# Two graph layers on one core: parts of a threshold search moved from VectorE to GpSimd, and the work between the two steps dealt in another order

## The chip, the core and the metric

The kernel runs on one core of a Trainium2 chip. The metric is the device time of one launch in microseconds (us); smaller is better. TensorE multiplies, VectorE (DVE in the rows) and ScalarE (ACT) do elementwise work and reductions, GpSimd (POOL) does small elementwise work and issues some DMAs, and SyncE (SP) issues the other DMAs. Each engine takes its instructions in the order of the program; between engines there are only semaphores.

## The reference

`x` is 3327 x 256, `adj` is a sparse symmetric 3327 x 3327 matrix. All is float32.

```python
h = relu(layernorm(x))
S = adj + eye
Rf = S / rowsum(S);  Rb = S / colsum(S)[:, None]
Xf = Xb = Xa = h;  Z = 0
for s in range(2):                       # step one, step two
    logits = (Xa @ W1) @ W2 @ (Xa @ W3).T
    # per row: keep the largest logits until their softmax mass reaches 0.9,
    # then softmax over the kept ones
    A = nucleus_softmax(logits, 0.9)
    Xf = Rf @ Xf;  Xb = Rb @ Xb;  Xa = A @ Xa
    Z += Xf @ U1[s] + Xb @ U2[s] + Xa @ U3[s]
x = x + layernorm(h + Z) * gamma + beta
h = relu(layernorm(x))
x = x + attention(h)                     # second layer, 8 heads
```

## The kernel before

Rows are padded to 3328 and cut into 26 tiles of 128 rows (t = 0 to 25). A step works through the tiles one after another, with tile t + 1 being begun while tile t is searched and tile t - 1 is used. For every tile, in a step:

- TensorE makes the logits (L1100), ScalarE copies them to SBUF (L1344), VectorE takes the row's maximum (`row_max`, L1871 in step two), ScalarE the exponentials (L1351).
- ScalarE probes two thresholds over the whole row (`probe`, L1404 and L1410, twice each) and signals `searched_early` at the end (L1433 in step two). In step two a bracket (its ends are the pairs `high` and `deep`, each a threshold and the excess mass there) is tightened with the first probe by GpSimd (`bracket`, L1724 to L1733) and with the second by VectorE.
- VectorE searches on: `start_search` makes the next candidate from the bracket, `bisect(t, k)` weighs the mass above the candidate in one pass over the row (`weigh`, L1928; three passes in step one, five in step two), and moves the candidate by a step from a small table (`steps_of`). In step two the pass k = 0 is followed by `narrow` (L1935 to L1942), and GpSimd makes the table (`make_steps`, L1738). In step one VectorE makes the table itself (`spans`, L1881), right before the first pass.
- `threshold` (L1967 to L1992) finds the exact threshold among the largest 24 values below the candidate; `sum_larger` (L1997 to L2000) signals `larger_summed`. GpSimd then counts (`count_needed`, L1743 to L1755), ScalarE counts ties (L1451) and lifts the row (L1457), GpSimd settles (`settle`: L1760, L1763 signals `settled`, L1766 signals `totalled`), and VectorE, which waits for both, makes the kept row (`keep`, L2109 to L2117).
- TensorE transposes the kept row and multiplies it with the features, and multiplies the adjacency tile (L1118).

VectorE's order in step two, from tile 2 on, is: `start_search(t)`, `bisect(t, 0)`, `keep(t-1)`, `row_max(t+1)`, `bisect(t, 1)` to `bisect(t, 4)`, `threshold(t)`, `sum_larger(t)`. GpSimd's order is `prepare(t+1)`, `bracket(t+1)`, `count_needed(t)`, `settle(t)`, `make_steps(t+1)`, then three DMA issues that add the tile's results to z in HBM.

**Between the steps** lies a stage of 26 slots. In slot t TensorE transposes a tile (L763) and multiplies it with U1 and U2 (L777, eight matmuls, into two PSUM banks of four), ScalarE scales the second bank into `both` (L818, L819), and VectorE sums four scaled parts into z (`gather`, L853 to L861: two from the first bank, then two from `both`); GpSimd adds z to HBM with a DMA (L1803). TensorE may refill the first bank of slot t for slot t + 2 when L855 of slot t has run (`sides_read`), the second when L819 has (`both_ready`). Step two's tiles 0 and 1 are searched in between the slots, so all engines deal slots and passes by an order written out by hand. TensorE does tile 0's adjacency products (L1118) and the first logits there too.

## Time and profile before

| what | value |
|---|---|
| median of 3 runs | 2296.23 us (2295.15 to 2298.56) |
| the profiled execution | 2297.46 us |
| its span | 2295.7 us |
| mean granted TensorE clock | 0.983 of full speed |
| busy: TensorE, VectorE, ScalarE, GpSimd | 2140.1, 2042.6, 1935.1, 854.2 us |
| step one | about 60 to 900 us, 32.2 us a tile |
| between the steps | about 1005 to 1155 us |
| step two after it | about 1155 to 2220 us, 42.75 us a tile |

Busy time alone doesn't say which engine sets the end: TensorE is busy most, but the chain that ended last can run through another. A row of the timeline gives the start, the length, the engine, the line, and in square brackets how long the engine had been idle before it and what ended that.

### The profile page before, as it was taken

What the parts mean: (1) busy time and instruction counts of PE and PEld (TensorE: products, weight loads), DVE (VectorE), ACT (ScalarE), POOL (GpSimd) and SP (SyncE); (2) the same over time, 40 slices, a digit from 0 to 9 for tenths busy, and PEclk for the clock granted to TensorE, in tenths of its full rate; (3) what the DMA queues carried; (4) which work ended last, traced back from release to release, by engine and by line L of the source; (5) the groups of instructions that cost most, each with busy time, mean ns of one, the idle gap of its engine ahead of it and who ended that gap; (6) DMA issues with size and microseconds to landing.
All of it is one profiled execution on the core that took longest, in us unless ns stands there. A gap on an engine that the chain in (4) does not pass through costs nothing.

```text
span 2295.7 us, 26397 instructions
## 1 busy us (share of the span) xinstructions
PE 2140.1 (93%) x8282; PEld 1381.0 (60%) x8282; DVE 2042.6 (89%) x3758; ACT 1935.1 (84%) x2831; POOL 854.2 (37%) x1233
## 2 busy tenths in 40 slices
PE   7599999999999998998899999999999999999987
PEld 4377777777777777543355555555555555555556
DVE  5699999999999998138859999999999999999996
ACT  5899999999999996258379989989989999899844
POOL 2134443344334442003224444444444444444420
PEclk9699999999999999999999999999999999999998
DMA  7255544554455543332322112112212212122242
GB/s 247 79 124 138 113 98 112 129 115 110 101 124 129 114 100 72 105 99 42 54 56 57 39 52 57 44 48 57 52 40 56 52 42 54 52 44 52 54 124 72
DMA packets 85168, 190.05 MB, mean 83 GB/s; under 512 B 12193, under 2 KB 65056, under 8 KB 85024
## 3 DMA queue, kind: packets, MB, share of 16 engines
q0 software_dynamic: 26208, 61.37, 17.1%
q1 hardware_dynamic: 56496, 125.48, 16.5%
q10 hardware_dynamic: 2320, 1.48, 0.2%
q8 instruction: 67, 1.10, 0.2%
q14 instruction: 77, 0.63, 0.1%
HBM read 154.19 MB, written 34.10 MB: 82 GB/s over the span
## 4 chain that ended last, share of the span: by engine, by line
DVE 45%; PE 4%; issue 1%; POOL 0%; ACT 0%; DVEq 0%; ACTq 0%; POOLq 0%
DVE junk L1928 19%; DVE small L1975 4%; DVE logits L1967 4%; DVE logits L2117 4%; DVE small L1871 4%; PE bank L1118 2%; DVE small L1956 1%; DVE small L1959 1%; PE bank L777 1%; DVE small L1980 1%; DVE small L1983 1%; DVE QT L2031 1%; PE bank L1181 1%; PE bank L1144 0%; PE bank L1100 0%
## 5 line engine op out<-in xcount | busy, mean ns | idle before, releaser
L1928 DVE SCALAR_TENSOR_TENSOR junk<-logits,small,expd 128x3327 uint8<-128x3327 f32 x184 | 677.9, 3684 | 4.7
L1144 PE MATMUL bank<-h_aug,turns 128*128 128x256 f32 x2704 | 628.2, 379 | 0.0
L1118 PE MATMUL bank<-both,pair 128*128 128x512 f32 x1352 | 611.2, 596 | 17.8 <-ACT sides L1497 17.8
L1144 PEld LDWEIGHTS bank<-h_aug,turns 128*128 128x128 f32 x2704 | 498.4, 190 | 94.5 <-issue 30.1
L1118 PEld LDWEIGHTS bank<-both,pair 128*128 128x128 f32 x1352 | 251.0, 190 | 302.6 <-issue 261.0
L1118 PE MATMUL bank<-h_aug,both 128*128 128x257 f32 x1352 | 316.6, 384 | 2.8 <-ACT sides L1480 1.6
L1118 PEld LDWEIGHTS bank<-h_aug,both 128*128 128x128 f32 x1352 | 250.9, 190 | 64.5 <-issue 26.9
L1100 PE MATMUL bank<-KTr,QT 64*128 64x512 f32 (+1 forms) x728 | 246.5, 613 | 43.7 <-ACT logits L1344 39.8
L1404 ACT ACTIVATE junk<-expd,small 128x3327 int8<-128x3327 f32 x88 | 270.1, 3069 | 1.5
L1410 ACT ACTIVATE junk<-expd,small 128x3327 int8<-128x3327 f32 x88 | 270.5, 3073 | 0.3
L1473 ACT ACTIVATE turns<-bank 128x512 f32<-128x512 f32 (+1 forms) x364 | 188.7, 562 | 52.0 <-PE bank L1134 46.5
L1134 PE MATMUL bank<-ident,logits 128*128 128x128 f32 x1352 | 190.8, 277 | 39.6 <-DVE logits L2117 29.4
L1743 POOL TENSOR_TENSOR small<-small 128x1 f32<-128x1 f32 x52 | 14.5, 278 | 571.5 <-DVE small L2000 571.5
L1134 PEld LDWEIGHTS bank<-ident,logits 128*128 128x128 f32 x1352 | 159.8, 141 | 100.2 <-DVE logits L2117 39.9
L1975 DVE MAX8 small<-logits 128x8 f32<-128x416 f32 (+1 forms) x416 | 209.9, 578 | 0.0
L1451 ACT ACTIVATE junk<-logits,small 128x3327 int8<-128x3327 f32 x52 | 159.4, 3066 | 49.1 <-DVE small L1992 49.1
L1100 PEld LDWEIGHTS bank<-KTr,QT 64*128 64x128 f32 x728 | 90.0, 188 | 182.5 <-ACT logits L1344 104.4
L1967 DVE SCALAR_TENSOR_TENSOR logits<-logits,small,expd 128x3327 f32<-128x3327 f32 x44 | 162.6, 3695 | 1.5
L1351 ACT ACTIVATE expd<-logits,small 128x3327 f32<-128x3327 f32 x44 | 135.0, 3069 | 34.0 <-DVE small L1873 33.9
L1344 ACT ACTIVATE logits<-bank 128x512 f32<-128x512 f32 (+1 forms) x286 | 145.4, 575 | 20.7 <-PE bank L1100 20.6
L2117 DVE SCALAR_TENSOR_TENSOR logits<-logits,small,expd 128x3328 f32<-128x3328 f32 x42 | 154.7, 3684 | 4.8 <-DVE small L2114 0.5
L1708 POOL TENSOR_SCALAR small<-small 128x1 f32<-128x1 f32 x52 | 40.9, 787 | 264.4 <-ACT expd L1351 243.1
(263 smaller groups left out, 3097.8 us busy)
## 6 DMA issues: line engine op xcount, KB each, us to landing
both<-adj_turned SPq DMA_DIRECT2D x52, 832.0 KB, 6.8
both<-adj_turned POOLq DMA_DIRECT2D x52, 832.0 KB, 9.3
pair<-adj_turned SPq DMA_DIRECT2D x52, 832.0 KB, 4.5
z<-sides POOLq DMA_DIRECT2D x78, 128.0 KB, 3.2
spread<-sides POOLq DMA_DIRECT2D x26, 128.5 KB, 3.6
turns<-spread SPq DMA_DIRECT2D x26, 128.5 KB, 2.1
attended<-att_out SPq DMA_DIRECT2D x26, 128.0 KB, 8.5
expd<-attended SPq DMA_DIRECT2D x26, 128.0 KB, 2.1
```

The costliest lines, as they stand in the source:

```text
L1100: pe.matmul(logits_bank(i)[:, 0:w], QT[r:r + DA, bass.ts(t, P)], keys_of(n, w), start=True, stop=True).then_inc(sem["logits_done"], 1)
L1118: done = pe.matmul(SX[:, 0:width], half(t, h)[:, bass.ts(jj, P)], rows_of(j), start=(j == 0), stop=(j == T - 1))
L1134: last = pe.transpose(TB[i % NTB][:, bass.ts(b, P)], kept[:, bass.ts(g + b, P)], ident[:, :])
L1144: last = pe.matmul(AB[:, 0:D], attT[i % 4][:, b, :], h_aug[:, g + b, 0:D], start=(g + b == 0), stop=(g + b == T - 1))
L1404: chain.did(act.activation(junk2[:, 0:N], e, ACT.Relu, bias=at, scale=-0.5, accum_out=col(t, "tail")))
L1410: chain.did(act.activation(junk2[:, 0:N], e, ACT.Sign, bias=at, scale=-0.5, accum_out=col(t, "side")))
L1451: act.activation(junk2[:, 0:N], me, ACT.Sign, bias=col(t, "tau"), scale=-1.0, accum_out=col(t, "less")).then_inc(sem["ties_counted"], 1)
L1473: act.activation(attT[i % 4][:, 0:w, :], TB[i % NTB][:, 0:w * P].rearrange("q (b r) -> q b r", r=P), ACT.Relu).then_inc(sem["turned_stored ...
L1928: chain.did(dve.scalar_tensor_tensor(junk[:, 0:N], logits[t % 3][:, 0:N], col(t, "cand"), expd[t % NE][:, 0:N], ALU.is_gt, ALU.mult, accum ...
L1967: chain.did(dve.scalar_tensor_tensor(me[:, 0:N], logits[t % 3][:, 0:N], col(t, "cand"), expd[t % NE][:, 0:N], ALU.is_le, ALU.mult, accum_o ...
L1975: chain.did(dve.max(winners(t)[:, 8 * n:8 * n + 8], me[:, at:min(at + NP // SEGMENTS, N)]))
L2117: dve.scalar_tensor_tensor(kept, kept, col(t, "sharetau"), expd[t % NE][:, :], ALU.add, ALU.min).then_inc(sem["kept_ready"], 1)
```

## The change

Five things, in the words of the code:

1. In step two the bracket's second tightening goes from VectorE to GpSimd (`close_bracket`, nine operations in four dependent groups). VectorE's `start_search` waits for `closed` and begins with the reciprocal. The first three tightening operations change places.
2. In step two `narrow` goes to GpSimd, nine operations in four dependent groups with the table's at the end. It waits for `weighed`, the end of the pass k = 0; VectorE waits for `steps_ready` ahead of the pass k = 1.
3. In step one GpSimd makes the table of steps (`make_steps`), after `prepare`; VectorE waits for it behind its first pass.
4. Between the steps ScalarE begins z: a third operation in its slot, from `both` in SBUF, which waits for its own L819 and for the z buffer to be free. VectorE's `gather` has three operations instead of four and waits for `z_begun`.
5. Between the steps VectorE's list has tile 1's start after slot 16 as before, but its passes k = 0, 1, 2 and `keep(0)` stand two slots apart.

```diff
@@ store_products(t), ScalarE
                act.activation(both[:, t, D:2 * D], bank[:, D:2 * D], ACT.Copy, scale=col_inv[:, t:t + 1]
                               ).then_inc(mid["both_ready"], 1)
+                act.wait_ge(mid["both_ready"], t + 1)
+                if t < 4:
+                    act.wait_ge(mid[f"z_stored{t}"], stores_in(t))
+                else:
+                    act.wait_ge(mid[f"z_added{t % 4}"], t // 4 * 16)
+                act.activation(z_out[t % 4], both[:, t, 0:D], ACT.Copy, scale=row_inv[:, t:t + 1]
+                               ).then_inc(mid["z_begun"], 1)
@@ gather(t), VectorE
-                dve.wait_ge(mid["products_done"], 2 * t + 1)
...
-                chain.did(dve.tensor_scalar(z, sides[:, 0:D], row_inv[:, t:t + 1], None, ALU.mult))
+                dve.wait_ge(mid["z_begun"], t + 1)
+                chain.did(dve.scalar_tensor_tensor(z, sides[:, 0:D], row_inv[:, t:t + 1], z, ALU.mult, ALU.add))
...
-                dve.wait_ge(mid["both_ready"], t + 1)
-                chain.did(dve.scalar_tensor_tensor(z, both[:, t, 0:D], row_inv[:, t:t + 1], z, ALU.mult, ALU.add))
-                chain.wait()
@@ GpSimd; move_ends holds the eight operations of bracket, which now calls it
+                    def close_bracket(t):
+                        high, deep = pair(t, "high"), pair(t, "deep")
+                        pool.wait_ge(sem["searched_early"], t + 1)
+                        move_ends(t, pair(t, "point1"), high, deep)
+                        pool.tensor_tensor(pair(t, "width"), deep, high, ALU.subtract).then_inc(sem["closed"], 1)
+
+                    def narrow(t):
...
+                        pool.wait_ge(sem["weighed"], t + 1)
+                        pool.wait_ge(sem["closed"], t + 1)
+                        chain.did(pool.tensor_tensor(up, deep, high, ALU.add))
+                        chain.did(pool.tensor_scalar(col(t, "move"), col(t, "mass"), col(t, "target"), None, ALU.is_ge))
+                        chain.did(pool.tensor_tensor(bottom, point, deep, ALU.subtract))
+                        chain.did(pool.tensor_scalar(half, pair(t, "width", 0), -0.5, None, ALU.mult))
+                        chain.wait()
+                        chain.did(pool.tensor_scalar(excess, point, -2.0, up, ALU.mult, ALU.add))
+                        chain.did(pool.tensor_scalar(col(t, "cand"), bottom, -0.5, col(t, "cand"), ALU.mult, ALU.add))
+                        chain.wait()
+                        chain.did(pool.tensor_scalar(moved, excess, col(t, "move"), bottom, ALU.mult, ALU.add))
+                        chain.did(pool.tensor_scalar(col(t, "cand"), half, col(t, "move"), col(t, "cand"),
+                                                     ALU.mult, ALU.add))
+                        chain.wait()
+                        pool.tensor_scalar(steps_of(t), constants[:, 4:4 + 2 * late], moved, None, ALU.mult
+                                           ).then_inc(sem["steps_ready"], 1)
 
                     def make_steps(t):
...
+                        pool.wait_ge(sem["low_ready"], t + 1)
+                        pool.tensor_scalar(steps_of(t), constants[:, 4:4 + 2 * late], col(t, "low"), -0.5 ** early,
+                                           ALU.mult, ALU.mult).then_inc(sem["steps_ready"], 1)
@@ GpSimd's list, between the steps and then per tile
+                            if t == 7:
+                                close_bracket(0)
                             if t == 8:
-                                make_steps(0)
+                                pool.wait_ge(sem["setup"], 2 * late)
+                                narrow(0)
...
                             if t == 15:
+                                close_bracket(1)
                                 count_needed(0)
                             if t == 16:
                                 settle(0)
-                                make_steps(1)
+                                narrow(1)
...
                             prepare(t + 1)
-                            if not first_step:
+                            if first_step:
+                                make_steps(t + 1)
+                            else:
                                 bracket(t + 1)
+                                close_bracket(t + 1)
                         if first_step or t > 0:
                             count_needed(t)
                             settle(t)
                             if not first_step and t + 1 < T:
-                                make_steps(t + 1)
+                                narrow(t + 1)
@@ VectorE's list between the steps
                         sum_larger(0)
-                        slot(15)
+                        slots(15, 17)
                         start_search(1)
-                        slot(16)
+                        slot(17)
                         bisect(1, 0)
-                        slot(17)
+                        slots(18, 20)
+                        keep(0)
+                        slot(20)
                         bisect(1, 1)
-                        slot(18)
-                        keep(0)
-                        slot(19)
+                        slots(21, 23)
                         bisect(1, 2)
-                        slots(20, T)
+                        slots(23, T)
                         bisect(1, 3)
```

VectorE's instructions in step two, at the start of a tile's search (`sum_larger` of the tile before is L2000), before:

```order
L2000 SCALAR_TENSOR_TENSOR small<-small,s_ones 128x24
L1896 TENSOR_SCALAR s_mask<-small 128x1
L1897 TENSOR_SCALAR s_mask<-small 128x1
L1900 COPY_PREDICATED small<-s_mask,small 128x2
L1901 COPY_PREDICATED small<-s_mask,small 128x2
L1903 TENSOR_TENSOR small<-small 128x2
...
L1906 RECIPROCAL small<-small 128x1
```

and in the changed kernel, where L1920 is the reciprocal of `start_search`, L1938 the pass k = 0 and L2107 the first instruction of `keep`:

```order
L1998 SCALAR_TENSOR_TENSOR small<-small,s_ones 128x24
L1920 RECIPROCAL small<-small 128x1
L1922 TENSOR_SCALAR small<-small 128x1
L1925 TENSOR_SCALAR small<-small 128x1
L1927 SCALAR_TENSOR_TENSOR small<-small 128x1
L1930 SCALAR_TENSOR_TENSOR small<-small 128x1
L1933 TENSOR_SCALAR small<-small 128x1
L1938 SCALAR_TENSOR_TENSOR junk,small<-logits,small,expd 128x3327
L2107 RECIPROCAL small<-small 128x1
```

The six operations ahead of the reciprocal, two behind L1933 and the five of `narrow` behind the pass are gone from VectorE.

GpSimd's instructions at the same place in the changed kernel, from the end of `count_needed` (L1777) over `settle` (L1782 to L1788) and `narrow` (L1743 to L1755) to the first DMA; before, `settle` was followed by L1738 alone and then by the DMA:

```order
L1777 TENSOR_SCALAR small<-small 128x1
L1782 TENSOR_SCALAR small<-small 128x1
L1785 TENSOR_SCALAR small<-small 128x1
L1788 TENSOR_SCALAR small<-small 128x1
L1743 TENSOR_TENSOR small<-small 128x1
L1744 TENSOR_SCALAR small<-small 128x1
L1745 TENSOR_TENSOR small<-small 128x1
L1746 TENSOR_SCALAR small<-small 128x1
...
L1755 TENSOR_SCALAR small<-s_constants,small 128x10
L1803 DMA z<-sides 128x256
```

So the queue behind `settle` has eight more instructions ahead of the DMAs.

VectorE's instructions between the steps in the changed kernel, from tile 1's pass k = 0 to `keep(0)` (L2107): slots 18 and 19 stand between them with three operations on z each, where before there were slot 17, the pass k = 1 and slot 18.

```order
L1938 SCALAR_TENSOR_TENSOR junk,small<-logits,small,expd 128x3327
L847 TENSOR_SCALAR row_sum<-turns 128x1
L849 RECIPROCAL row_inv<-row_sum 128x1
L856 SCALAR_TENSOR_TENSOR sides<-bank,row_inv,sides 128x256
L858 SCALAR_TENSOR_TENSOR sides<-bank,col_inv,sides 128x256
L861 SCALAR_TENSOR_TENSOR sides<-both,col_inv,sides 128x256
L847 TENSOR_SCALAR row_sum<-turns 128x1
...
L2107 RECIPROCAL small<-small 128x1
```

The passes moved back in the list; the slots moved forward.

## Rows read from the trace of the kernel before

**Rows 1.** The page's chain that ended last, shares of the span by engine

```profile
DVE 45%; PE 4%; issue 1%; POOL 0%; ACT 0%; DVEq 0%; ACTq 0%; POOLq 0%
```

**Rows 2.** Busy us (x instructions) by engine in one stretch of step two

```profile
1400.00:1500.00 100.00, 96.74 (x333) 55.61 (x332) 96.28 (x184) 90.50 (x132) 45.02 (x70) 1.00 0.21 51
```

**Rows 3.** Timeline of VectorE in step two: start, length, engine, line, operation

```profile
1410.61 0.15 DVE L1896 TENSOR_SCALAR s_mask<-small 128x1 int32<-128x1 f32 x1
...
1411.45 0.16 DVE L1906 RECIPROCAL small<-small 128x1 f32<-128x1 f32 x1
...
1412.92 3.69 DVE L1928 SCALAR_TENSOR_TENSOR junk<-logits,small,expd 128x3327 uint8<-128x3327 f32 x1
...
1417.47 0.16 DVE L2109 RECIPROCAL small<-small 128x1 f32<-128x1 f32 x1
...
1418.12 3.69 DVE L2117 SCALAR_TENSOR_TENSOR logits<-logits,small,expd 128x3328 f32<-128x3328 f32 x1
1421.72 3.61 DVE L1871 TENSOR_REDUCE small<-logits 128x1 f32<-128x3327 f32 x1
```

**Rows 4.** Timeline of GpSimd over the same stretch

```profile
1411.68 0.27 POOL L1748 TENSOR_SCALAR small<-small 128x1 f32<-128x1 f32 x1
1412.04 0.23 POOL L1751 TENSOR_SCALAR small<-small 128x1 f32<-128x1 f32 x1
...
1412.57 0.23 POOL L1755 TENSOR_SCALAR small<-small 128x1 f32<-128x1 f32 x1
1413.67 3.12 POOL L1760 TENSOR_SCALAR small<-small 128x1 f32<-128x1 f32 x1 [0.87 <-ACT junk L1451]
1416.88 0.29 POOL L1763 TENSOR_SCALAR small<-small 128x1 f32<-128x1 f32 x1
1417.28 0.34 POOL L1766 TENSOR_SCALAR small<-small 128x1 f32<-128x1 f32 x1
```

**Rows 5.** Timeline of step one, a reduction on VectorE and GpSimd beside it

```profile
527.81 2.29 DVE L1856 TENSOR_REDUCE small<-logits 128x1 f32<-128x2048 f32 x1
528.81 0.31 POOL L1760 TENSOR_SCALAR small<-small 128x1 f32<-128x1 f32 x1
```

**Rows 6.** Timeline of GpSimd, first and last of `bracket`'s eight operations

```profile
1186.47 0.22 POOL L1724 TENSOR_SCALAR small<-small 128x1 f32<-128x1 f32 x1 [9.36 <-ACT small L1433]
1188.10 0.20 POOL L1733 TENSOR_TENSOR small<-small 128x2 f32<-128x2 f32 x1
```

**Rows 7.** Timeline of ScalarE in step two: the second probe's last operation

```profile
1450.04 0.39 ACT L1433 ACTIVATE small<-small 128x1 f32<-128x1 f32 x1
```

**Rows 8.** Timeline of step one, VectorE and ScalarE

```profile
523.13 0.21 DVE L1889 TENSOR_SCALAR small<-small 128x1 f32<-128x1 f32 x1
523.25 0.22 DVE L1881 TENSOR_SCALAR small<-s_constants,small 128x6 f32<-128x6 f32 x1
523.51 3.69 DVE L1928 SCALAR_TENSOR_TENSOR junk<-logits,small,both 128x3327 uint8<-128x3327 f32 x1
...
532.07 3.07 ACT L1351 ACTIVATE expd<-logits,small 128x3327 f32<-128x3327 f32 x1 [0.24 <-DVE small L1873]
```

**Rows 9.** Timeline of VectorE between the steps: tile 0's search begins, and tile 2's

```profile
1051.86 0.15 DVE L1896 TENSOR_SCALAR s_mask<-small 128x1 int32<-128x1 f32 x1 [2.90 <-ACT small L1433]
...
1195.81 0.16 DVE L1896 TENSOR_SCALAR s_mask<-small 128x1 int32<-128x1 f32 x1 [13.14 <-ACT small L1433]
```

**Rows 10.** Groups by line, 1000 to 1160 us: count, busy us, mean ns, idle before

```profile
L853 DVE TENSOR_SCALAR sides<-bank,row_inv 128x256 f32<-128x256 f32 x26 | 12.6, 483 | 6.3 <-PE bank L777 6.0 <-DVE row_inv L842 0.3
L819 ACT ACTIVATE both<-bank,col_inv 128x256 f32<-128x256 f32 x26 | 12.2, 471 | 0.0
```

**Rows 11.** Timeline of TensorE between the steps

```profile
1111.57 3.60 PE L777 MATMUL bank<-logits,turns 128*128 128x512 f32 x8
...
1121.93 5.37 PE L777 MATMUL bank<-logits,turns 128*128 128x512 f32 x8 [2.66 <-DVE sides L855]
...
1128.42 1.96 PE L777 MATMUL bank<-logits,turns 128*128 128x512 f32 x4 [0.91 <-DVE sides L855]
```

87 lines of the change are left out of this document (25 added, 62 removed).

## The prediction

> **What bounds the kernel now.** I read the chain that ended last first: 45% of the span on VectorE against 4% on TensorE [rows 1], although TensorE is busier. It reaches back only to the stage between the steps, so step one has to be judged by who waits there. The busy times of a stretch of step two show VectorE at 96.28 of 100 us and TensorE at 96.74 [rows 2]: the first has no listed idle time in a tile's 42.75 us, only the small gaps between dependent instructions, the second has some 1.4 us a tile left. So VectorE sets step two's pace, and TensorE lies close behind. In step one ScalarE waits 0.24 us for VectorE in each tile, just ahead of the exponentials [rows 8]: VectorE sets the pace there too. Between the steps the engines wait for each other in turn: TensorE waits for VectorE's slots [rows 11], VectorE for ScalarE's probe [rows 9].
>
> **Step one.** The table of steps is one VectorE operation, 523.25 to 523.47, and the pass starts 0.04 later, at 523.51 [rows 8]. Without it the pass follows L1889, which ends at 523.34, so at 523.38: 0.13 us less. GpSimd makes the table right after `prepare`, most of a tile ahead of its use, so that costs nothing; its cover is most of a 32 us tile, and if it were gone VectorE would wait out one small operation. ScalarE's 0.24 us become 0.11, still above zero. 26 tiles x 0.13 = **3.3 us**. From below: nothing, if ScalarE's 0.24 were not slack at all.
>
> **Step two, what VectorE sheds.** At the start of a search the six operations ahead of the reciprocal take 1410.61 to 1411.45, 0.84 us, and the two behind L1919 hold the pass back by 0.13, by the same step as in step one [rows 3, 8]: the pass starts at 1411.95 instead of 1412.92. Behind the pass, from its end (1416.61) to `keep` (1417.47) lie 0.86 us, nearly all of it `narrow` [rows 3]. Together 1.8 us a tile. Most of it doesn't arrive, and this is the core of the forecast.
>
> **What is late next: `settle`.** `keep` waits for `settled`. GpSimd's L1760 took 3.12 us, from 1413.67 to 1416.79, and the pass on VectorE ended at 1416.61 [rows 3, 4]. The same L1760 took 0.31 us beside a row reduction [rows 5]. So a VectorE pass with two operands in SBUF holds back a GpSimd operation begun under it, a reduction doesn't. The Trainium skill says this in "SBUF — State Buffer", section "Who interferes with whom": the two share a port as an exclusive lock, a Vector instruction with two SBUF inputs shuts out a GpSimd one that reads SBUF, `tensor_reduce` never does. By that rule the trace agrees, with 3.12 against 0.31 us.
>
> Now replay GpSimd with the pass at 1411.95. `count_needed` is released by `sum_larger`, which doesn't move. L1748 begins at 1411.68 and gets through; L1751 would begin at 1412.04 [rows 4], 0.09 us after the pass, and is held until the pass ends at 1411.95 + 3.69 = 1415.64, so it ends near 1415.7. From L1751's end to L1755's end are 0.53 us (1412.27 to 1412.80): 1416.25. L1760 starts 0.1 later with 0.31 us of its own: 1416.65. L1763 ended 0.38 after L1760 (1416.79 to 1417.17): 1417.03, and `keep` begins 0.1 us behind that, at 1417.13 instead of 1417.47. `totalled` follows 0.45 after `settled`, as before, so the kept row's own start stays 0.65 behind `keep`: 1417.78 instead of 1418.12. Of 1.8 us, **0.34** arrive; about 1.4 become a wait of VectorE ahead of `keep`, in which the pass is over and GpSimd is free.
>
> **Do the new GpSimd chains come in time?** `narrow` begins behind L1766, near 1417.5. One group of four gets in partly before the kept row's 3.69 us; the rest runs from 1421.5 on, under the row maximum, a reduction that ends at 1425.3 [rows 3]. Eight operations in three groups took 1.83 us [rows 6], so what is left needs some 2 us of 3.8. `close_bracket` has the eight and one more, 2.2 us with the signal; the second probe ends at 1450.43 [rows 7], so `closed` comes at 1452.7, while the reciprocal would want to start at 1410.61 + 42.75 = 1453.36. Both hidden, with 1.8 and 0.7 us to spare. The DMAs behind `narrow` go out some 5 us later; their readers stand one tile on. If a cover goes, the excess is paid in full.
>
> Tile 2's search waits 13.14 us for ScalarE anyway [rows 9]; there `close_bracket` stands open (2.2 instead of 0.84 us) and `narrow`'s going pays it back, so I take nothing. Tiles 3 to 25: 23 x 0.34 = **7.8 us**.
>
> **Between the steps.** A slot of VectorE loses one operation of 0.48 and its gap, 0.52 us [rows 10]. A slot of ScalarE gains one; no row shows it, so 0.38 (small operations nearby, an estimate: L1433's 0.39 [rows 7]) to 0.47 (L819 [rows 10]), and 0.15 for waiting on L819: about 0.5. Five such slots (3 to 7) lie ahead of tile 0's second probe, for which VectorE already waits 2.90 us at 1051.86 [rows 9]. That search begins 5 x 0.5 + (2.2 - 0.84) = 3.8 us later. Seven slots at 0.52 and `narrow`'s 0.8, less about 1 us for a first `steps_ready` that nothing covers, win back nearly that much by slot 14; TensorE's product 16, which waits for slot 14, comes 0.3 later.
>
> Then the dealing. TensorE waited 2.66 us for slot 18, and the eight matmuls behind took 5.37 us instead of 3.60 [rows 11]: 1.2 GHz for part of them after the idle time, where full clock gives 3.60. Slot 19 cost 0.91 more. Together 2.66 + 1.77 + 0.91 = 5.3 us. With the first pass behind slot 17 and two slots from pass to pass, VectorE needs 2 x 1.74 + 4.3 = 7.8 us for two slots and a pass (1.74: three operations of 0.48 on z with their gaps and 0.2 to 0.3 for the row's inverse; 4.3: the pass of 3.69 and two small operations behind it; both estimates from those rows [rows 3, 10]), TensorE 2 x 3.65 = 7.3 (3.60 less its overlap, and two transposes): slots 18 to 22 are read in time, and only the product after the third pass waits, for about 1.1. 5.3 - 1.1 - 0.3 = **3.9 us**. From there TensorE's products lead to the first logits, and these to step two, so it arrives. Bounds: 0 if the new waits fall so that two more products run at the lower clock, 6 if the early part costs nothing.
>
> **Sum.** 3.3 + 7.8 + 3.9 = 15.0. The profiled execution took 2297.46, which gives 2282.5; the median lies 1.2 below that execution, so **2281.5**.
>
> **Rivals.**
>
> A. *`settle` slips through earlier.* If the pass starts 0.1 us later than I have it, L1751 runs and only L1754 and L1755 are held; `settled` comes 0.3 us sooner. 23 x 0.3 = 7 more: 2274.5. For it: only 0.09 us lie between. Against it: the two starts are as regular as clockwork from tile to tile. 0.17.
>
> B. *Moving work to GpSimd buys nothing in step two.* If L1748 is held as well, `settled` is 0.36 later and the 0.34 us are gone; the same if `close_bracket` is slowed by more than its 0.7 us, as VectorE's small two-operand instructions run beside it. Then 3.3 + 3.9 remain: 2289. The Trainium skill warns of it in "Perfetto Trace Analysis", section "Optimizing Scalar/DVE Operations": as the two share a read port, moving operations between them might not help. Here the trace agrees for most of it, with 1.4 of 1.8 us. 0.15.
>
> C. *ScalarE's share of z costs TensorE.* `sides_read` now needs ScalarE too, which sits in 3 us probes. If two or three more products wait as long as the 2.66 us and run at the lower clock, 6 us are lost instead of 3.9 won: 2291.5. For it: the waits of 2.66 us [rows 11]. Against it: `both_ready` tied TensorE to ScalarE already. 0.12.
>
> D. *The table of steps comes late* (slower). One place: VectorE ahead of the pass k = 1. It decides once `narrow` needs more than the 3.8 us under the row maximum, or is held there after all. Then its 2 us stand open: 23 x (2 - 0.34) = 38 lost, 7 won: 2327. Against it: 0.31 us beside the reduction [rows 5]. 0.06.
>
> The forecast itself 0.5, own range 2277 to 2286.
>
> **Numbers.** A measurement here can tell about 0.2%, 4.6 us: faster is below 2291.6. The forecast, A, B and half of C are faster: 0.84, which I take down to 0.81 for parts that add up against me; same 0.12, slower 0.07. The range reaches from A's 2273 to C's 2292.
>
> **What would show it.** Right: in step two a period of 42.4 us, no small VectorE operations around the pass, a wait of about 1.4 us ahead of `keep` for GpSimd, its L1751 successor about 3.6 us long; step one's tile 0.13 shorter; no wait of TensorE at slots 18 and 19. Wrong: VectorE waiting for `closed` or for `steps_ready` in steady tiles, or products at the lower clock behind slot 20.

## The result and the profile after

The changed kernel takes 2277.32 us in the median (2276.47 to 2278.12, 4 runs), the kernel before 2295.81 beside it (2295.15 to 2298.56, 4 runs): ratio 0.9917, 95% interval 0.9905 to 0.9928, 18.5 us less. The prediction was 2281.5 us, range 2273 to 2292. Sign and range held; the two terms of step one and step two were both mis-sized, in opposite directions.

First the page of the changed kernel: busy time by engine, and the chain that ended last by engine.

```profile
PE 2137.1 (94%) x8282; PEld 1379.3 (61%) x8282; DVE 1987.0 (87%) x3368; ACT 1947.4 (86%) x2857; POOL 1137.5 (50%) x1701
DVE 74%; PE 8%; issue 6%; POOL 4%; ACT 4%; DMA 0%; DVEq 0%; SPq 0%; ACTq 0%; POOLq 0%
```

VectorE lost 56 us of work, GpSimd gained 283, much of it waiting that the profile counts as busy: a held small operation is listed with 3.4 us. GpSimd now has 4% of the chain [rows 1].

Where the time went can be read from how far apart the same instructions stand in the two profiled executions. The row maximum of step two (L1871 before, L1902 after) gives it: the rows list the instructions of one line from 1190 us on, with their durations in ns and the first and the last start; before, then after. The first start is tile 3's, the last tile 25's.

```profile
L1871 DVE TENSOR_REDUCE small<-logits x23: 3609/3610/3619, 1207.9 to 2148.5; 128x1 f32<-128x3327 f32 x23
```

```profile
L1902 DVE TENSOR_REDUCE small<-logits x23: 3603/3604/3606, 1201.5 to 2125.9; 128x1 f32<-128x3327 f32 x23
```

940.6 us became 924.4 over 22 tiles: 42.75 became 42.02 a tile, 0.74 less, where the prediction had 0.34. The rest, by the same reading:

| stretch of the profiled executions | before | after | difference |
|---|---|---|---|
| to step one's last search | 877.7 | 876.7 | -1.0 |
| from there to tile 0's row maximum | 139.8 | 136.9 | -2.9 |
| tile 0's row maximum to tile 2's (the slots) | 146.4 | 143.2 | -3.2 |
| tile 2's row maximum to tile 3's | 44.0 | 44.7 | +0.7 |
| 22 tiles of step two | 940.6 | 924.4 | -16.2 |
| behind the last row maximum | 147.2 | 148.8 | +1.6 |

The second line is not the change's: it touches nothing there, and in the experiments below, which share that code, the same stretch took 136.8 to 140.4 us. The third line is loose too: kernels that are alike between the steps (runs 9 and 10 below) took 143.1 and 142.0 us there. The profiled pair is 21 us apart; the runs say 18.5.

Now a steady tile of step two in the changed kernel, VectorE from the last small operation ahead of the pass k = 0 to the row maximum [rows 3]:

```profile
1444.20 0.21 DVE L1933 TENSOR_SCALAR small<-small 128x1 f32<-128x1 f32 x1
1444.45 3.70 DVE L1938 SCALAR_TENSOR_TENSOR junk<-logits,small,expd 128x3327 uint8<-128x3327 f32 x1
1448.08 0.08 DVE L1938 DVE_READ_ACCUMULATOR junk<-logits,small,expd 128x1 f32 x1
1449.26 0.16 DVE L2107 RECIPROCAL small<-small 128x1 f32<-128x1 f32 x1 [1.11 <-POOL small L1785]
...
1449.97 3.73 DVE L2115 SCALAR_TENSOR_TENSOR logits<-logits,small,expd 128x3328 f32<-128x3328 f32 x1
1453.63 3.60 DVE L1902 TENSOR_REDUCE small<-logits 128x1 f32<-128x3327 f32 x1
```

and GpSimd over the same stretch [rows 4]: the end of `count_needed` (L1770 to L1777), `settle` (L1782, L1785), then `narrow`.

```profile
1444.13 0.27 POOL L1770 TENSOR_SCALAR small<-small 128x1 f32<-128x1 f32 x1
1444.49 0.23 POOL L1773 TENSOR_SCALAR small<-small 128x1 f32<-128x1 f32 x1
1444.81 3.43 POOL L1776 TENSOR_SCALAR small<-small 128x1 f32<-128x1 f32 x1
1448.21 0.23 POOL L1777 TENSOR_SCALAR small<-small 128x1 f32<-128x1 f32 x1
1448.54 0.31 POOL L1782 TENSOR_SCALAR small<-small 128x1 f32<-128x1 f32 x1
1448.94 0.29 POOL L1785 TENSOR_SCALAR small<-small 128x1 f32<-128x1 f32 x1
...
1450.04 0.20 POOL L1745 TENSOR_TENSOR small<-small 128x1 f32<-128x1 f32 x1
1450.19 3.60 POOL L1746 TENSOR_SCALAR small<-small 128x1 f32<-128x1 f32 x1
...
1455.28 0.34 POOL L1755 TENSOR_SCALAR small<-s_constants,small 128x10 f32<-128x10 f32 x1
```

The reader is to see three things. VectorE waits 1.11 us ahead of `keep`, for `settled`. L1773, which the prediction had held, began 0.04 us behind the pass and ran in 0.23 us, and so it did in all 23 tiles from tile 3 on; the next, L1776, is held to the pass's end in each of them. `narrow` is held in the same way under the kept row and is done 1.8 us ahead of its reader.

### The profile page after: what moved, and what is told of

Its sections match the earlier page's. It is cut to its first block, busy times and chain, and to the rows that moved or that the text cites. A ratio compares the mean times of both kernels' runs of the same rounds, so it can differ in the third digit from the quotient of the medians.

```text
span 2274.7 us, 26450 instructions
## 1 busy us (share of the span) xinstructions
PE 2137.1 (94%) x8282; PEld 1379.3 (61%) x8282; DVE 1987.0 (87%) x3368; ACT 1947.4 (86%) x2857; POOL 1137.5 (50%) x1701
## 4 chain that ended last, share of the span: by engine, by line
DVE 74%; PE 8%; issue 6%; POOL 4%; ACT 4%; DMA 0%; DVEq 0%; SPq 0%; ACTq 0%; POOLq 0%
DVE junk L1938 28%; DVE small L1973 9%; DVE logits L1965 8%; DVE logits L2115 8%; DVE small L1902 4%; DVE small L1887 3%; DVE small L1954 2%; PE bank L754 2%; PE bank L777 2%; DVE small L1957 2%; DVE small L1978 2%; POOL small L1776 1%; DVE small L1981 1%; DVE logits L1894 1%; PE bank L1110 1%
## 5 line engine op out<-in xcount | busy, mean ns | idle before, releaser
L1938 DVE SCALAR_TENSOR_TENSOR junk<-logits,small,expd 128x3327 uint8<-128x3327 f32 x184 | 678.2, 3686 | 8.1 <-POOL small L1755 3.5
L1719 POOL TENSOR_SCALAR small<-small 128x1 f32<-128x1 f32 x52 | 34.1, 656 | 256.7 <-ACT small L1425 256.7
L1343 ACT ACTIVATE expd<-logits,small 128x3327 f32<-128x3327 f32 x44 | 135.1, 3071 | 18.5 <-DVE small L1904 18.3
```

The costliest lines, as they stand in the source:

```text
L1938: return dve.scalar_tensor_tensor(junk[:, 0:N], logits[t % 3][:, 0:N], col(t, "cand"), expd[t % NE][:, 0:N], ALU.is_gt, ALU.mult, accum_ou ...
```

## The experiments

Theory S, which is the prediction's core: in step two `settled` is what ends late. A GpSimd operation that begins behind the start of a two-operand pass of VectorE waits out the pass, so `settled` comes as many small groups behind the pass's end as are left when it begins, and what is taken off VectorE is worth only what it moves that. Several of the expectations call it theory L. A group is a set of GpSimd operations that don't depend on each other; each group waits for the one before. The rivals are named run by run. Each run was timed beside the kernel before; the ratios compare with 0.9917.

**1. The bracket's ends back on VectorE.**

```diff
@@ close_bracket, GpSimd
-   move_ends(t, pair(t, "point1"), high, deep)
-   pool.tensor_tensor(pair(t, "width"), deep, high, ALU.subtract).then_inc(sem["closed"], 1)
+   pool.sem_inc(sem["bracketed"], 1)
@@ start_search, VectorE: the six operations ahead of the reciprocal, as before
+   chain.did(dve.copy_predicated(high, mask[:, 0:1].to_broadcast([P, 2]), here))
...
+   dve.tensor_tensor(pair(t, "width"), deep, high, ALU.subtract).then_inc(sem["closed"], 1)
```

> The changed kernel with the bracket's last move given back to VectorE (the six small operations ahead of the reciprocal); narrow stays on GpSimd. Theory S (settle is what ends late): the pass k = 0 starts 0.86 us later in a tile of step two, but then all of count_needed gets through ahead of it, so settled comes only 0.26 us later (pass end + 0.5 instead of pass end + 1.1), and the tile goes from 42.0 to 42.3 us: 23 x 0.26 = 6 us, less about 1 between the steps, so some 5 us more than the changed kernel, near 2282.5, ratio 0.9943. Rival N (the gain of step two is narrow's, which lay on the path behind the pass; the earlier pass buys nothing): no difference from the changed kernel, 2277. Rival P (every operation shed counts): 0.86 x 23 = 20 us more, near 2297.

Measured: 2280.85 us, ratio 0.9928 (0.9915 to 0.9942), 2.5 us above the changed kernel by the ratios. The tile takes 42.27 us, 0.25 more; tile 0's row maximum to tile 2's takes 140.7 instead of 143.2. All of `count_needed` now runs ahead of the pass, and one operation is held:

```profile
1443.87 0.22 POOL L1776 TENSOR_SCALAR small<-small 128x1 f32<-128x1 f32 x1
1445.04 2.91 POOL L1781 TENSOR_SCALAR small<-small 128x1 f32<-128x1 f32 x1 [0.94 <-ACT junk L1444]
1448.04 0.29 POOL L1784 TENSOR_SCALAR small<-small 128x1 f32<-128x1 f32 x1
```

The pass now starts 2.11 us behind the last accumulator of `sum_larger`, where it was 1.32. So 0.79 us of VectorE's work cost 0.25: theory S, and neither N (nothing) nor P (all of it). The size in total was a miss: between the steps 2.5 us came back, not 1. Tile 0's search accounts for 1.5 of them; the other 1.0 comes at slot 16, where runs 9 and 10, which are alike there, differ by 1.2.

**2. `narrow` back on VectorE.**

```diff
@@ bisect, k = 0, VectorE
-   weigh(t).then_inc(sem["weighed"], 1)
+   chain.did(weigh(t))
+   chain.wait()
+   narrow(t)          # the five operations of before; two more stand ahead of the pass again
@@ narrow, GpSimd
+   pool.wait_ge(sem["narrowed"], t + 1)   # and then the table alone
```

> The changed kernel with narrow given back to VectorE (with the two differences ahead of the pass; GpSimd only makes the table); the bracket's ends stay on GpSimd. Theory S: VectorE waits 1.1 us for settled behind the pass anyway, and narrow's 0.86 us fit into that wait. The pass starts 0.13 later, so 0.1 us a tile, 3 us in 23 tiles; the last tile loses its 2.1 us wait for the table and pays 0.9, and tile 0 does the same: about 2 less. Near 2278.5, ratio 0.9926; the wait ahead of keep is 0.2 to 0.3 us. Rivals N and P: 0.86 to 1.0 us a tile, 20 to 23 us more, near 2298.

Measured: 2280.01 us, ratio 0.992 (0.9907 to 0.9934), within the measurement of the changed kernel. The tile takes 42.23 us, 0.21 more and not 0.1. VectorE's timeline, from `narrow`'s last operation to the kept row:

```profile
1451.34 0.21 DVE L1936 SCALAR_TENSOR_TENSOR small<-small 128x1 f32<-128x1 f32 x1
1451.97 0.16 DVE L2113 RECIPROCAL small<-small 128x1 f32<-128x1 f32 x1 [0.42 <-POOL small L1769]
```

`narrow` lies whole in the wait for `settled`, with 0.42 us left. What its move to GpSimd bought in a steady tile is only the 0.2 us by which small operations ahead of the pass no longer hold it back: the same group is the first one held in both kernels, so `settled` moves with the pass, one for one. The move also costs at the ends: with `narrow` on VectorE the last tile is 2.0 us shorter (146.8 us behind the last row maximum instead of 148.8), and the stretch from tile 0's row maximum to tile 2's took 1.4 us less (141.8, of which 1.0 comes at the same slot 16), against 4.6 us lost in 22 tiles. Rivals N and P are out: they gave 20 us.

**3. z begun by VectorE again.**

```diff
@@ store_products, ScalarE
-   act.activation(z_out[t % 4], both[:, t, 0:D], ACT.Copy, scale=row_inv[:, t:t + 1]).then_inc(mid["z_begun"], 1)
@@ gather, VectorE: four operations, as before
+   chain.did(dve.tensor_scalar(z, sides[:, 0:D], row_inv[:, t:t + 1], None, ALU.mult))
```

> The changed kernel with z begun by VectorE again, as in the kernel before; all else as changed. Theory E (the slots pass the work from one busy engine to another): VectorE's slots 0.52 us longer, ScalarE's 0.5 shorter, VectorE no longer waits 36 us for ScalarE's z; tile 0's probes come 2.5 us sooner, seven slots of VectorE cost 3.6: within 2 us of the changed kernel, 2277 (2275 to 2279). Rival V (VectorE's slots were the bound, so z on ScalarE is worth 0.5 us a slot from slot 8 on): some 6 to 9 us more, near 2284. Rival C (ScalarE's z costs TensorE waits): 4 us less, 2273.

Measured: 2277.99 us, ratio 0.991 (0.9896 to 0.9923). From tile 0's row maximum to tile 2's it takes 143.1 us, against 143.2. Theory E: the move is worth nothing that can be seen. ScalarE's z operation takes 0.51 us, VectorE's took 0.48, and between the steps VectorE waits 36 us for it.

**4. The old dealing.**

```diff
@@ VectorE's list between the steps: pass, keep and slots in the order of before
-   slots(15, 17); start_search(1); slot(17); bisect(1, 0); slots(18, 20); keep(0); slot(20); bisect(1, 1)
+   slot(15); start_search(1); slot(16); bisect(1, 0); slot(17); bisect(1, 1); slot(18); keep(0); slot(19)
```

> The changed kernel with tile 1's search, passes and keep(0) dealt among the slots as in the kernel before. Theory K (as predicted): TensorE waits for slots 18 and 19 again, 2.7 + 0.9 us, and the eight matmuls behind the first wait take 1.8 us more at the lower granted clock; with the wait that the later dealing has (1.36 us) gone, about 4 us more than the changed kernel, 2281, ratio 0.9936. Rival Z (z on ScalarE has shortened the slots so far that the old dealing does as well): no difference, 2277, and no wait of TensorE over 1 us there.

Measured: 2282.4 us, ratio 0.9932 (0.9918 to 0.9945), 3.4 us above the changed kernel; the stretch takes 147.2 instead of 143.2 us. TensorE's timeline has the two waits of the kernel before [rows 11], the first with 4.29 us instead of 2.66:

```profile
1119.49 5.08 PE L777 MATMUL bank<-logits,turns 128*128 128x512 f32 x8 [4.29 <-DVE sides L858]
1125.44 3.67 PE L777 MATMUL bank<-logits,turns 128*128 128x512 f32 x8 [0.65 <-DVE sides L858]
```

The granted clock from 1119 to 1125 us is 0.72 of full, where the changed kernel has 1.00. Theory K; 4.0 us for the dealing by the profiles and 3.4 by the runs, where the prediction had 3.9 net of what the early part loses. One word on the change: in the kernel before, as in this run, tile 1's search begins behind slot 15; in the changed kernel it begins behind slot 16, so it too stands one slot later.

**5. A reduction in place of the first pass.**

```diff
@@ bisect, k = 0, step two
-   weigh(t).then_inc(sem["weighed"], 1)
+   dve.tensor_reduce(col(t, "mass"), logits[t % 3][:, 0:N], AX.X, ALU.max).then_inc(sem["weighed"], 1)
```

> The changed kernel, but the first pass of step two's search is a row reduction (tensor_reduce, one operand, 3.6 us) in place of the two-operand pass of 3.7 us; the mass it should find is not computed, so the thresholds of step two are not the reference's, while the count and length of all other instructions stay. Theory L (a two-operand pass holds GpSimd's operations back, a reduction doesn't): the operation of count_needed that took 3.43 us takes 0.2 to 0.3, settled is there before the pass ends, and VectorE's 1.1 us wait ahead of keep is gone. The kept row can then start when ScalarE's lift is done, 0.8 us sooner; TensorE has only 0.5 us a tile left, so the tile goes from 42.0 to 41.5 us: 22 x 0.5 = 11 us less, near 0.987 of the kernel before. Rival G (GpSimd's chain is late of itself, whatever VectorE does): the long operation stays long or the wait stays, 42.0 us a tile, 0.9917.

This kernel leaves out the mass that the pass should find. Measured: 2258.22 us, ratio 0.9826 (0.9811 to 0.9841). GpSimd's timeline, under a reduction from 1442.55 to 1446.17:

```profile
1442.91 0.24 POOL L1776 TENSOR_SCALAR small<-small 128x1 f32<-128x1 f32 x1
1443.11 0.22 POOL L1777 TENSOR_SCALAR small<-small 128x1 f32<-128x1 f32 x1
1444.29 0.31 POOL L1782 TENSOR_SCALAR small<-small 128x1 f32<-128x1 f32 x1 [0.95 <-ACT junk L1443]
1444.69 0.29 POOL L1785 TENSOR_SCALAR small<-small 128x1 f32<-128x1 f32 x1
```

L1776 takes 0.24 us in place of 3.43, in all 22 tiles of the stretch, and `settled` is there 1.2 us ahead of the reduction's end. That is theory L as clearly as it can be had. The Trainium skill says in "SBUF — State Buffer", section "Who interferes with whom", that on this chip `tensor_reduce` never contends with GpSimd; the trace agrees. The expectation was wrong on what comes next: it let TensorE stop the gain at 0.5 us a tile, and it is 0.83 (41.19 us a tile). The kept row now waits for ScalarE's lift, the only wait of VectorE that is listed in a steady tile:

```profile
1447.26 3.69 DVE L2116 SCALAR_TENSOR_TENSOR logits<-logits,small,expd 128x3328 f32<-128x3328 f32 x1 [0.64 <-ACT logits L1449]
```

**6. One more small group on GpSimd.**

```diff
@@ count_needed, behind the first subtraction of need
+   if not first_step:
+       chain.did(pool.tensor_scalar(col(t, "spare"), col(t, "need"), 1.0, 0.0, ALU.mult, ALU.add))
+       chain.wait()
```

> The changed kernel with one more small operation in step two's count_needed, on which the next one waits (0.3 us more on GpSimd; its result is used by nothing). Theory L: the operation that now begins 0.04 us after the pass and gets through begins 0.3 us after it and is held to the pass's end; one group more is left to run behind the pass, so settled comes 0.35 us later and the tile takes 42.35 instead of 42.0: 23 x 0.35 = 8 us more than the changed kernel, ratio 0.995. Rival G (the 0.3 us are absorbed while the pass runs, as the chain has 3.7 us of pass to run in): no difference, 0.9917.

Measured: 2285.74 us, ratio 0.9948 (0.9935 to 0.9962), 7 us above the changed kernel. VectorE's wait ahead of `keep` went from 1.11 to 1.42 us, the tile from 42.02 to 42.33:

```profile
1447.96 3.48 POOL L1776 TENSOR_SCALAR small<-small 128x1 f32<-128x1 f32 x1
1451.53 0.24 POOL L1779 TENSOR_SCALAR small<-small 128x1 f32<-128x1 f32 x1
```

L1776, which is the changed kernel's L1773, now begins 0.31 us behind the pass (1447.65) and is held. One operation, 0.3 us with its gap and ahead of a wait of 3.5 us, is paid in full.

**7. `count_needed` shortened.**

```diff
@@ count_needed
+   pool.wait_ge(sem["tau_ready"], t + 1)
+   chain.did(pool.tensor_tensor(col(t, "floor"), col(t, "target"), col(t, "negabove"), ALU.add))
+   chain.did(pool.tensor_scalar(col(t, "negtau"), col(t, "tau"), -1.0, None, ALU.mult))
+   chain.wait()
+   pool.wait_ge(sem["gt_summed"], t + 1)
+   chain.did(pool.tensor_tensor(col(t, "need"), col(t, "floor"), col(t, "gt"), ALU.subtract))
...
-   chain.did(pool.tensor_tensor(col(t, "need"), col(t, "target"), col(t, "have"), ALU.subtract))
-   chain.wait()
...         # -tau no longer stands in the last group
@@ sum_larger, VectorE: the sum of the larger values now signals by itself
+   dve.scalar_tensor_tensor(kept, v, col(t, "tau"), v, ALU.is_gt,
+                            ALU.mult, accum_out=col(t, "gt")).then_inc(sem["gt_summed"], 1)
```

> The changed kernel with GpSimd's count_needed shortened: target + negabove and -tau are computed as soon as tau is there, the first subtraction starts when the larger values are summed, 0.23 us ahead of their count, and one group of dependent operations falls away. Theory L: the last group of count_needed then starts no later than 0.05 us after the pass and gets through; only settle's first operation is held. Settled comes 0.5 us behind the pass's end instead of 1.1, the tile takes 41.5 us: 22 x 0.5 = 11 us less than the changed kernel, ratio 0.987. If the last group starts 0.1 us or more after the pass, it is held, and only 0.2 us a tile are won, 4.5 us, ratio 0.990. Rival G: GpSimd's chain ends a third of a us sooner while the pass still runs, nothing is won: 0.9917.

Measured: 2281.14 us, ratio 0.9929 (0.9916 to 0.9943), 42.14 us a tile: a miss on both counts, 2.8 us slower than the changed kernel.

```profile
1444.97 0.19 POOL L1775 TENSOR_SCALAR small<-small 128x1 f32<-128x1 f32 x1
1445.25 3.62 POOL L1777 TENSOR_SCALAR small<-small 128x1 f32<-128x1 f32 x1
1448.96 0.23 POOL L1780 TENSOR_SCALAR small<-small 128x1 f32<-128x1 f32 x1
1449.34 0.31 POOL L1785 TENSOR_SCALAR small<-small 128x1 f32<-128x1 f32 x1 [0.15 <-POOL small L1780]
```

The two early operations come only when tau is there, 0.15 us before the sum of the larger values, and hold the first subtraction back until 0.5 us behind it. So the chain reached its last but one group (L1777) only 0.15 us behind the pass (1445.10): held, and the last group (L1780), which in the changed kernel is the held one, now comes behind the pass. So one group more is paid behind the pass. It costs less than in run 6, since the held operation has no companion any more: from its end to the start of `settle`'s second operation are 0.88 us (1448.87 to 1449.75), where the changed kernel has 0.70 (1448.24 to 1448.94), and the tile is 0.12 longer. The theory isn't touched; the timing of GpSimd's queue was wrong, since an "early" operation was taken for a free one.

**8. Step one: the wait for the table ahead of the pass.**

```diff
@@ bisect
-   if n == 0 and not first_step:
+   if n == 0:
        dve.wait_ge(sem["steps_ready"], t + 1)
    chain.did(weigh(t))
-   if n == 0 and first_step:
-       dve.wait_ge(sem["steps_ready"], t + 1)
```

> The changed kernel with step one's wait for the table of steps ahead of the first pass, as in step two, instead of behind it. Theory W: the wait for a second semaphore behind the pass is what took back half of step one's gain, as the first small operation starts 0.19 us behind the pass instead of 0.12; moved ahead of the pass it costs nothing or 0.03, so 0.04 to 0.07 us a tile, 26 x 0.06 = 1.6 us less than the changed kernel, ratio 0.991, and step one's tile takes 32.08 us. Rival A: ScalarE sets step one's pace once VectorE is 0.08 us shorter, and nothing moves: the tile stays at 32.14 us.

Measured: 2276.75 us, ratio 0.9906 (0.9891 to 0.9921). From the start of one search to the next, a steady tile of step one takes 32.06 us, against 32.12 in the changed kernel and 32.20 before. So the 0.07 us by which VectorE starts earlier behind the pass arrive: theory W. The whole stretch hides it, with 771.4 us from tile 1's search to tile 25's against 771.9 in the changed kernel and 773.3 before. The reason is one interval, from tile 1's search to tile 2's: 33.8 us here and 32.7 in the changed kernel, and over the 14 profiles anything from 32.4 to 33.8, with no order in it by the code of step one. Run 10 has the same edit and the same steady tile, 32.05 us, where run 9 without it has 32.12.

From 130 to 880 us the sum of the waits for VectorE above 0.2 us, ahead of ScalarE's exponentials, is 5.2 us before, 3.5 after, and one of 0.3 here:

```profile
ACT expd L1343 <- DVE small L1904: 0.3, 1, 0.3
```

The waits didn't go, they fell below what is listed: the median gap there is 0.24 us before, 0.16 after and 0.10 here. So ScalarE still waits for VectorE, and rival A, by which ScalarE sets the pace, is out.

**9. `settle` on VectorE in step two**, the version that the experiments pointed to.

```diff
@@ count_needed, GpSimd, step two
+   pool.wait_ge(sem["tau_ready"], t + 1)
+   chain.did(pool.tensor_scalar(col(t, "negtau"), col(t, "tau"), -1.0, None, ALU.mult))
...         # the first three groups as before
+   pool.tensor_scalar(col(t, "need"), col(t, "need"), TO_INTEGER, -TO_INTEGER,
+                      ALU.add, ALU.add).then_inc(sem["counted"], 1)
+   return          # settle, on GpSimd, returns at once
@@ keep, VectorE
-   dve.wait_ge(sem["settled"], t + 1)
-   chain.did(dve.reciprocal(col(t, "invties"), col(t, "negties")))
+   dve.wait_ge(sem["ties_counted"], t + 1)
+   dve.wait_ge(sem["counted"], t + 1)
+   chain.did(dve.tensor_scalar(col(t, "negties"), col(t, "less"), col(t, "beyond"), -1.0, ALU.subtract, ALU.min))
+   chain.did(dve.tensor_scalar(col(t, "need"), col(t, "need"), 1.0, -1.0, ALU.max, ALU.mult))
...         # count, 1 / negties, total, sharetau, 1 / total: three more groups
```

> The changed kernel with settle, and the last operation of count_needed, on VectorE in step two (GpSimd keeps the first four groups of count_needed, whose last one gets through in the changed kernel, 0.04 us behind the pass's start). Theory L: nothing that keep needs is held under the pass any more. Behind the pass come four groups of small operations on VectorE at 0.25 us, so the kept row starts 1.1 us behind the pass's end instead of 1.8; ScalarE's lift allows 1.0. So 0.7 us a tile, 42.0 becomes 41.3, 22 x 0.7 = 15 us less than the changed kernel, ratio 0.985, and VectorE waits for no one in a steady tile. Rival W (every small operation counts on VectorE, the engine that sets the pace; the wait comes back elsewhere, at TensorE or for the table of steps): 42.0 us a tile, 0.9917. Rival H (the last group left on GpSimd starts a little later and is held, then waits out the pass): 0.3 us a tile, 0.989.

Measured: 2264.22 us, ratio 0.9854 (0.9839 to 0.9869). The tile takes 41.50 us.

```profile
1441.80 3.70 DVE L1947 SCALAR_TENSOR_TENSOR junk<-logits,small,expd 128x3327 uint8<-128x3327 f32 x1
1445.42 0.08 DVE L1947 DVE_READ_ACCUMULATOR junk<-logits,small,expd 128x1 f32 x1
1445.42 0.20 DVE L2022 TENSOR_SCALAR small<-small 128x1 f32<-128x1 f32 x1
...
1446.80 3.69 DVE L2138 SCALAR_TENSOR_TENSOR logits<-logits,small,expd 128x3328 f32<-128x3328 f32 x1
```

No listed wait of VectorE is left in a steady tile. The kept row starts 1.30 us behind the accumulator's end, where it was 1.81; from the first small operation to the row it is 1.38 us for four groups, 0.35 each rather than the expected 0.25, which is why the tile stands at 41.5 and not 41.3. TensorE is listed as busy for 907.02 of the 909 us from 1205 on, so it is close behind; run 5 shows that at least 0.3 us a tile more would be to be had from it.

**10. The same, with run 8's edit to step one.**

```diff
@@ bisect, as in run 8, on top of run 9
-   if n == 0 and not first_step:
+   if n == 0:
```

> The kernel of the run before (settle on VectorE in step two) with step one's wait for the table of steps ahead of the first pass as well. Theory L: another 0.5 to 1.5 us, ratio 0.9845. Rival W: 0.991.

Measured: 2262.85 us, ratio 0.9848 (0.9835 to 0.9862). The fastest version here that computes the whole reference. Its lead over run 9 is smaller than the runs can tell, though the steady tile of step one shows it (run 8).

**11. Run 9 with the bracket's ends on VectorE**, so run 1 without the wait for `settled`.

```diff
@@ the edit of run 1, on top of run 9
+   dve.tensor_tensor(pair(t, "width"), deep, high, ALU.subtract).then_inc(sem["closed"], 1)
```

> The kernel with settle on VectorE, with the bracket's last move given back to VectorE as well, as in the first run of this study. There it cost 0.25 us a tile, as the wait for settled took the rest. Theory S: without that wait the 0.86 us count in full, 22 x 0.86 = 19 us, less the 3 us that the bracket on GpSimd costs between the steps and in tile 2: 16 us more than the kernel with settle on VectorE, ratio 0.9925, 42.35 us a tile. Rival Q (the price of the bracket on VectorE is 0.25 us a tile whatever ends late, for instance because ScalarE or TensorE sets the pace): 3 us more, ratio 0.987.

Measured: 2281.18 us, ratio 0.9925 (0.9911 to 0.9938). The tile takes 42.27 us, 0.77 more than in run 9, where the same edit cost 0.25 in run 1. The edit is the same and so is its work: it puts off the pass by 0.78 us here (2.11 instead of 1.33 us behind the last accumulator of `sum_larger`), by 0.79 in run 1. What differs is what ends late. Rival Q is out.

**12. The kernel before, with `settle` on VectorE.**

```diff
@@ on the kernel before: count_needed and keep as in run 9
+   dve.wait_ge(sem["counted"], t + 1)
```

> The kernel before, with nothing changed but settle and the last operation of count_needed, which go to VectorE in step two. Theory S: there narrow, on VectorE, ended later than settled, so settle was off the path; its groups now come behind narrow, 1.3 us instead of the 0.65 that keep's own small operations took: 23 x 0.65 = 15 us slower than the kernel before, ratio 1.0065, 43.4 us a tile. Rival L2 (the held operation on GpSimd was late in the kernel before too, so taking it off helps): 5 to 8 us faster, 0.997.

Measured: 2315.62 us, ratio 1.0077 (1.0064 to 1.0091), 43.53 us a tile. VectorE's timeline, from the last operation of `narrow` over the first of `settle` to the kept row:

```profile
1420.48 0.22 DVE L1951 SCALAR_TENSOR_TENSOR small<-small 128x1 f32<-128x1 f32 x1
1420.79 0.21 DVE L2024 TENSOR_SCALAR small<-small 128x1 f32<-128x1 f32 x1
...
1422.17 3.69 DVE L2140 SCALAR_TENSOR_TENSOR logits<-logits,small,expd 128x3328 f32<-128x3328 f32 x1
```

Behind `narrow` 1.38 us of small operations stand ahead of the kept row, where `keep` alone had 0.65 [rows 3]. The edit that makes the changed kernel 14 us faster makes the kernel before 18 us slower, for there `narrow` on VectorE covered `settle`.

## Why the prediction was right, and where it was off

**What bounds step two, and what is late next.** Right, and run 5 shows it without a detour: with a reduction for the pass, the held operation takes 0.24 us and the wait is gone. Runs 1, 2, 6, 9, 11 and 12 follow from the same rule, with prices of 0.25, 0.21, 0.31, -0.52, 0.77 and 0.78 us a tile. Run 7 was a wrong forecast of when GpSimd's operations begin, not of what happens to them.

**The replay of GpSimd under the pass, the step that failed in size.** The prediction had L1751's successor held because it would begin 0.09 us behind the pass. It began 0.04 behind and got through. GpSimd's chain stood 0.07 us earlier against VectorE's than in the kernel before: from the first small operation behind `sum_larger` to this one it is 1.43 us before (1410.61 to 1412.04 [rows 3, 4]) and 1.36 after (1443.13 to 1444.49). So one group of 0.33 us fewer was left behind the pass: the wait is 1.1 us, not 1.4, and the tile gains 0.74 instead of 0.34. This is rival A's mechanism, given 0.17, with its 0.3 us; it was not the pass that came later, as the prediction put it (the pass came where it was forecast, 1.32 us behind the last accumulator instead of 1.34), but the other side that came sooner. Why it did stays open. The first operation of `count_needed` begins 0.16 us behind that accumulator instead of 0.23, but so it does in every experiment except run 7, also in run 12, the kernel before with `settle` moved. The 22 tiles gave 16.2 us, where the term of 7.8 stood for 23.

**The new chains on GpSimd.** In steady tiles both came in time, as predicted: `narrow` with 1.8 us to spare, `close_bracket` with 0.5 (0.7 predicted). Not priced was the last tile, which has no row maximum to cover `narrow`:

```profile
2170.03 3.69 DVE L1938 SCALAR_TENSOR_TENSOR junk<-logits,small,expd 128x3327 uint8<-128x3327 f32 x1 [2.11 <-POOL small L1755]
```

That is the +1.6 us of the table's last line, and run 2 gets it back. Tile 2, for which the prediction took nothing, costs 0.7: the reciprocal of its search comes 1.4 us later against its row maximum, as the prediction's 2.2 instead of 0.84 says, and `narrow`'s going pays back only half of it.

**Step one.** 3.3 us predicted, 1.6 measured from the first search to the last. The pass does start 0.13 us earlier, but a steady tile gains only 0.07 of it. The rest goes where the wait for `steps_ready` now stands, behind the pass: the first small operation comes 0.19 us behind the accumulator's start instead of 0.12. The prediction let the gain arrive whole and gave that wait no price; run 8 moves it and gets its 0.07 back. The other bound that it named, ScalarE, was not reached.

**Between the steps.** 3.9 us predicted, 3.2 measured up to tile 2's row maximum, and 2.5 with tile 2's 0.7; differences of about 1 us can't be told there. The early part went as forecast: the reciprocal of tile 0's search comes 3.3 us later against that tile's row maximum (3.8 predicted), and by slot 14 all of it is won back, with TensorE's product 16 at 81.4 us behind that row maximum and at 81.6 before. The dealing alone is worth 4.0 (run 4). Handing z to ScalarE is worth nothing (run 3), and rival C's lost products aren't seen: TensorE's waits for VectorE between the steps sum to 14.1 us, 15.9 before. That the bracket on GpSimd has no cover at tile 0 was priced, with 1.4 us; run 1 shows 1.5.

**Sum.** 15.0 predicted, 18.5 measured. Step two came out 8.4 us above its term; step one, the stage between and the last tile some 5 us below theirs. The total was better than its parts: that it came within 4.2 us is in part luck, as the errors had opposite signs. Small slips in the sums on record: the median before less 15.0 is 2281.2, five slots and the bracket give 3.9 and not 3.8, rival A's own time is 2274.5 while the range starts at 2273, and the chances of the forecast, A, B and half of C add up to 0.88, not 0.84. None of them changes the verdict. Rival B (GpSimd buys nothing) holds for `narrow` in the total, but for another reason than the one given: not that GpSimd is slowed, but that most of the work lay in a wait, and the ends of the loop took back most of the rest.

## What to carry to other kernels

Taking work off the engine that sets the pace is worth what it moves of the next late signal. Find that signal first: if it is made by small GpSimd operations beside two-operand passes of VectorE, count how many dependent groups are left when the pass begins, because each is paid behind the pass. Work of VectorE ahead of the pass is paid in full as long as the same group is the first one held (run 2), and only in part where putting off the pass lets another group through (run 1); work behind the pass is free up to the end of the wait. Moving the few operations that make the signal to VectorE itself can gain as much again as relieving VectorE did (14 us here, on top of 18.5), but only once nothing longer covers them (run 12). And price the ends of the loop too: the first and last tiles lack the cover of the steady ones.

## What the runs showed of the hardware

- Whether a GpSimd operation is held is decided within 0.1 us around the pass's start, and the listed starts don't tell alone. In step two of the changed kernel L1773 began 0.03 to 0.04 us behind the pass in 23 tiles and always ran at once, in 0.23 to 0.24 us. L1745 began 0.06 to 0.07 us behind the kept row in 24 tiles and ran at once in eight of them, as at 1450.04 above; in the other 16 it was held:

```profile
1407.97 3.69 DVE L2115 SCALAR_TENSOR_TENSOR logits<-logits,small,expd 128x3328 f32<-128x3328 f32 x1
1408.04 3.67 POOL L1745 TENSOR_TENSOR small<-small 128x1 f32<-128x1 f32 x1
```

- But in step one the table of steps, L1760, began only 0.01 to 0.02 us behind a pass in 24 tiles and was held in every one. So the border differs from instruction to instruction; why stays open. Of the GpSimd operations seen at 0.08 to 0.20 us behind a pass in the 14 traces, all were held.

```profile
476.04 3.69 DVE L1938 SCALAR_TENSOR_TENSOR junk<-logits,small,expd 128x3327 uint8<-128x3327 f32 x1
476.06 3.73 POOL L1760 TENSOR_SCALAR small<-s_constants,small 128x6 f32<-128x6 f32 x1
```

- An operation that gets through costs VectorE a few hundredths of a us: the kept row took 3.73 to 3.74 us in the eight tiles in which L1745 ran at once, and 3.69 to 3.70 in the 16 others. Held operations are listed with 3.4 to 3.7 us.
- The Trainium skill ("SBUF — State Buffer", section "Who interferes with whom") calls the port that the two share an exclusive lock and says that the order of issue decides who blocks. The traces agree in that one of the two always waits for the other; that an operation listed as 0.04 us second ran at once, and VectorE's was the longer for it, shows that the order of issue is not quite the order of the starts in the trace.
